# Moving the gate-times-up product of the narrow stages from one engine to two others, in their first half

## The reference, cut to what matters

```python
x = x + 0.5 * L0_ffn(layernorm(x))    # "f0", stages 0 to 7
x = x + L0_attn(layernorm(x))         # "a0"
x = x + 0.5 * L0_ffn(layernorm(x))    # "f0", stages 8 to 15
x = x + 0.5 * L1_ffn(layernorm(x))    # "f1", stages 0 to 7
x = x + L1_attn(layernorm(x))         # "a1"
x = x + 0.5 * L1_ffn(layernorm(x))    # "f1", stages 8 to 15
```

```python
def fp4_quant_dequant(x):             # blocks of 16 along the last dimension
    scale = max(max|xb| / 6, 1e-12)
    return nearest_of(0, .5, 1, 1.5, 2, 3, 4, 6)(|xb / scale|) * sign(xb) * scale
def L0_ffn(x):                        # 256 -> 704 -> 256
    gate = fp4(x) @ fp4(w_gate).T;  y = fp4(x) @ fp4(w_up).T
    h = silu(gate) * y
    return fp4(h) @ fp4(w_down).T
```

## Time and profile before

| | |
|---|---|
| median of the three runs | 2735.21 us |
| the profiled execution | 2740.86 us, its span 2739.1 us |
| busy, share of the span | PE 87%, DVE 71%, ACT 60%, POOL 32% |
| mean granted TensorE clock | 0.955 of full speed |

### The profile page before, as it was taken

The page is one execution under the profiler, slowest core; times in us unless marked ns, Lnnn a source line. Parts: engine busy times, 40 slices in busy tenths (PEclk is TensorE's granted clock), DMA queues, the critical chain, the costliest instruction groups (busy, mean ns, idle before and its releaser), DMA issues.

```text
span 2739.1 us, 55707 instructions
## 1 busy us (share of the span) xinstructions
PE 2379.6 (87%) x23228; PEld 1832.4 (67%) x23228; DVE 1951.3 (71%) x3497; ACT 1645.2 (60%) x2731; POOL 876.0 (32%) x631
## 2 busy tenths in 40 slices
PE   1778878888998999889898998989898998988888
PEld 1456656665786787667675767767666786866767
DVE  6588998999897977857677767777777656353341
ACT  2244445555867665675656566766657667665654
POOL 0112111211332423153544444353526325422212
PEclk9799999998999999999999999999899998999999
DMA  4000000000000000000000000000000000000000
GB/s 161 19 1 1 1 1 1 1 1 1 1 1 1 1 1 14 11 13 13 13 13 14 13 14 13 2 13 13 13 21 13 21 9 1 9 1 9 9 9 9
DMA packets 34842, 32.89 MB, mean 12 GB/s; under 512 B 7648, under 2 KB 33952, under 8 KB 34592
## 3 DMA queue, kind: packets, MB, share of 16 engines
q1 hardware_dynamic: 34592, 29.33, 3.2%
HBM read 12.28 MB, written 4.19 MB: 6 GB/s over the span
## 4 chain that ended last, share of the span: by engine, by line
PE 61%; DVE 22%; ACT 7%; issue 5%; POOL 2%; SPq 2%; DMA 1%; POOLq 0%; DVEq 0%; ACTq 0%
PE psum L702 16%; PE psum L703 14%; PE psum L704 14%; PE psum L708 5%; PE psum L1134 2%; PE psum L1136 2%; PE psum L1135 2%; PE psum L985 2%; PE psum L1038 2%; DVE a1pr L1867 1%; PE psum L1015 1%; SPq L677 1%; ACT a1PT L1411 1%; DVE f0sc L1689 1%; POOL a1pr L2103 1%
## 5 line engine op out<-in xcount | busy, mean ns | idle before, releaser
L2116 POOL TENSOR_TENSOR f1hT<-f1g,f1hT 128x512 f16<-128x512 f32 x256 | 308.8, 1211 | 698.2 <-ACT f1hT L1512 698.0
L2103 POOL TENSOR_TENSOR a1pr<-a1PT,a1pr 128x1024 f16<-128x1024 f32 (+1 forms) x176 | 354.2, 2015 | 306.4 <-DVE a1pr L1867 306.3
L702 PE MATMUL psum<-f1sl,f1w1h 128*128 128x256 f16 x1024 | 285.1, 278 | 18.2 <-ACT f1g L1507 8.8
L702 PE MATMUL psum<-f1w2h,f1hT 128*128 128x256 f16 x1024 | 281.1, 274 | 5.2 <-POOL f1hT L2116 3.3
L703 PE MATMUL psum<-f1sl,f1w1h 128*128 128x256 f16 x1024 | 284.4, 278 | 0.0
L704 PE MATMUL psum<-f1sl,f1w1l 128*128 128x256 f16 x1024 | 284.3, 278 | 0.0
L704 PE MATMUL psum<-f1w2h,f1hT 128*128 128x256 f16 x1024 | 280.6, 274 | 0.0
L703 PE MATMUL psum<-f1w2l,f1hT 128*128 128x256 f16 x1024 | 280.5, 274 | 0.0
L1844 DVE TENSOR_REDUCE a1nm<-psum 128x2 f32<-128x768 f32 (+3 forms) x176 | 198.0, 1125 | 72.1 <-PE psum L965 71.7
L2092 POOL TENSOR_TENSOR f0h<-f0Y,f0sc 128x704 f32<-128x704 f32 x64 | 90.2, 1409 | 465.6 <-DVE f0Y L1704 465.5
L1867 DVE CAST a1pr<-a1PT 128x1024 f16<-128x1024 f32 (+1 forms) x176 | 162.3, 925 | 59.5 <-ACT a1PT L1411 45.3
(11 more groups left out here) (335 smaller groups left out, 7099.9 us busy)
## 6 DMA issues: line engine op xcount, KB each, us to landing
a1Q<-a1st SPq DMA_DIRECT2D x96, 64.0 KB, 2.6
a1K<-a1st SPq DMA_DIRECT2D x96, 64.0 KB, 2.6
x<-in_L_attn_x SPq DMA_DIRECT2D x8, 512.0 KB, 7.8
out<-x SPq DMA_DIRECT2D x8, 512.0 KB, 2.9
wslot<-in_L_ffn_w SPq DMA_DIRECT2D x1, 1024.0 KB, 9.6
wraw<-in_L_ffn_w SPq DMA_DIRECT2D x1, 1024.0 KB, 5.6
wslot<-in_L_ffn_slot_embeds SPq DMA_DIRECT2D x1, 1024.0 KB, 7.8
a1Q<-a1mr SPq DMA_DIRECT2D x64, 4.0 KB, 1.7
```

Of the source, the lines that this page charges most:

```text
L702: e.matmul(out, lh, rh, start=start, stop=False)
L2103: e.tensor_tensor(a1["pr"][:, i % 2, 1, :, 0:w], a1["PT"][:, i % 2, :, 0:w], a1["pr"][:, i % 2, 0, :, 0:w], ALU.subtract).then_inc(s["a1_pl"])
L2116: e.tensor_tensor(hT1[:, 1, 2 * hp:2 * hp + 2, :], gg[:, hp % 2, :, :], hT1[:, 0, 2 * hp:2 * hp + 2, :], ALU.subtract).then_inc(s["f1_hl"])
```

## The change

For stages with f < B (tiles 0 to 31) the DVE multiplication at line 1685 is left out. ACT gets a new piece, due at G + 3.4: after `f0_u` and the rounding of the tile two before (`f0_hy`), it copies the up product, scaled, from banks 2 and 3 to `f0M` and signals `f0_ue`, which now frees the banks. POOL gets a new generator `f0_inner`, due at G + 4.2, which multiplies `f0M` into `f0h` and signals `f0_th`. DVE keeps the waits on `f0_si` and `f0_u` at that place. For f >= B the multiplication stays on DVE, with one added wait on `f0_th`.

```diff
 # tensor, f0_gate
-                            banks.after(n, "f0_th", ft + 1)
+                            banks.after(n, "f0_ue" if f < B else "f0_th", ft + 1)
 # scalar, f0_hidden, after the silu
+                    if f < B:
+                        yield G + 3.4
+                        q.wait_ge("f0_u", ft + 1)
+                        q.wait_ge("f0_hy", ft - 1)
+                        e.activation(f0["M"][:, t % 2, :].rearrange("p (i n) -> p i n", i=2), psum[:, 2:4, 0:FH], ACT.Copy,
+                                     scale=1.0 / (XS * WS)).then_inc(s["f0_ue"])
 # vector, f0_hidden
                     yield G + 3.8
                     q.wait_ge("f0_si", ft + 1)
                     q.wait_ge("f0_u", ft + 1)
-                    e.scalar_tensor_tensor(h3, psum[:, 2:4, 0:FH], 1.0 / (XS * WS), h3, ALU.mult, ALU.mult).then_inc(s["f0_th"])
+                    if f >= B:
+                        q.wait_ge("f0_th", ft)
+                        e.scalar_tensor_tensor(h3, psum[:, 2:4, 0:FH], 1.0 / (XS * WS), h3, ALU.mult, ALU.mult).then_inc(s["f0_th"])
 # gpsimd, new
+            def f0_inner(f):
+                S = at_f0(f)
+                for t in range(NT):
+                    ft = 4 * f + t
+                    h = f0["h"][:, ft % 3, :]
+                    yield S + 10.0 + 10.0 * t + 4.2
+                    q.wait_ge("f0_si", ft + 1)
+                    q.wait_ge("f0_ue", ft + 1)
+                    e.tensor_tensor(h, f0["M"][:, t % 2, :], h, ALU.mult).then_inc(s["f0_th"])
...
+                  chain(f0_inner, B), *[chain(z, B) for z in (a0_powers, a1_powers, a1_probs)],
```

More of the change, by code:

```diff
@@ L2119, in gpsimd @@
             return [weights(), *[chain(z, 2 * B) for z in (f0_powers, f0_products, f0_hidden)],
-                  *[chain(z, B) for z in (a0_powers, a1_powers, a1_probs)],
+                  chain(f0_inner, B), *[chain(z, B) for z in (a0_powers, a1_powers, a1_probs)],
                   *[chain(z, 2 * B) for z in (f1_powers, f1_mlp)]]
```

## The result

The changed kernel took 2785.4 us (median; 2781.8 to 2788.2) beside 2736.6 for the kernel before: a ratio of 1.0189, 95% interval 1.0166 to 1.0212. Forecast was 2721 with a range up to 2748. It is slower by 49 us, outside the range, and of the other sign.

A forecast was written before the change was run, and what follows sets the result against it. DVE was taken to bound the kernel from 120 to 630 us. Removal 24.3 less port 9.0 leaves 15.3 us, of which 14 arrive: 2735.2 - 14 = 2721 us, range 2702 to 2748.

The forecast's parts named there:

- Where DVE is bound: 120 to 630 us, f0 beside a0: DVE waits 37.3 us, 7% of the stretch, so is taken for 93%.
- nine tenths of the sum arrive: Last step: a thinner DVE list waits a little more elsewhere, so 14 of 15.3 us saved reach the time.
- The cost on ACT: 32 copies of 128x704 from PSUM at 0.75 us, 24 us in all, covered by ACT's idle time.
- POOL's duration: 32 products of 128x704 from SBUF at 1.39 us, 44 us more on POOL, hidden; nearest row up to 1766 ns.
- The port: POOL products hold up DVE instructions reading two SBUF tensors, and the cast: 0.30 us each, 9.0 us, ends 0 and 33.
- rival 1: The port takes it back: each new product costs DVE 0.8 us, 24 us in all, giving 2735; chance 0.20.
- 24.3 us removed: Line 1685 leaves DVE's list for 30 tiles in the full stretch, at 0.81 us each.
- The chain: Up product to line 1689 grows 1.3 to 1.4 us per tile, hidden if DVE has other work; counted at nothing.
- Rival 2: DVE waits for POOL at line 1689 in each tile: 27 us slower, 2762, deciding from 0.51 us a tile; chance 0.13.
- The gain at the banks: ACT frees banks 2 and 3, where PE waited 6.7 + 3.1 us for line 1685; counted at nothing.
- The order behind: Stages after 630 us: time won earlier moves all that follows forward, if their order stays as it is.
- rival 3: Planner rewrites wide stages after 630 us: eight table loads more or fewer, 10 us, 2711 or 2731; chance 0.12.

The follow-up runs named there:

- e5: Kernel before, own order: for f < B DVE's product done on 16 of 704 columns only, nothing added on ACT or POOL; 2724.0 us beside 2730.9.
- e6: Kernel before, own order, product still on DVE: ACT's copy added for f < B, DVE's product waits for it; 2740.4 us, ratio 1.0043.
- e8: Changed kernel with planner delays after ACT 129 for 130 and DVE 108 for 110, lowest planned end of 182 tries; 2695.0 us, ratio 0.9875.
- e2: Instructions of the kernel before (product on DVE) in the order the planner wrote for the changed kernel; 2780.1 us, ratio 1.0178.
- e1: Instructions of the changed kernel, every engine keeping the order of the kernel before; 2763.1 us, ratio 1.0119.
- e7: As e6, plus a POOL product of 128x704 whose result nobody uses, ACT's absolute value waiting for it; 2755.4 us, ratio 1.0096.
- e3: Changed kernel with the planner's delay after an ACT instruction moved from 130 to 131, giving another order; 2733.4 us, ratio 1.000.
- e11: Kernel before with the planner stopped after two rounds of its ten; 2748.0 us, ratio 1.0061.

## Why the prediction was wrong

**Where DVE is bound.** Right in the rows, and wrong in what followed. DVE had something to issue for 93% of the stretch, but taking 22 us out of it (e5) won 7 in the timed runs, and at most 17. The step "from its 7% of waiting I take that nine tenths of the sum arrive" failed first, though by the traces it may hold nearly (17 of 22).

**The cost on ACT.** Its duration was right (0.757 for 0.75 us). Whether its cover was there is not shown: e6 lost 5 to 9 us where nothing was counted, but with a wait of DVE for the copy that the change does not have.

**POOL's duration.** 1.39 us was taken from a product whose second operand is a small scale repeated; two whole tiles took 1.68. The stated ceiling of 1766 ns held for the median, not for single ones (2224).

**The port.** Mis-sized: 9.0 us forecast, 16.0 more in the records of the changed kernel, 17.7 beside the new product, 0.59 us for each where 0.30 was taken. That is three quarters of rival 1's price of 0.8, and it does not go away with a better order (18.2 us in e8). Of the 24.3 us removed 8 are left by this term alone, and 3 when the changed kernel is set beside e2, which has its order. The mechanism was right; the kind of DVE instruction was drawn too narrowly. "No others" than those with two tensors from SBUF and the cast is not what the rows say: the old line 1657 scales a tile of 128x32 in place, has one tensor input, and took up to 874 ns in the kernel before and 1619 in the changed one, where its median is 182. It and its like are also why the prediction found 10.1 us of excess and the whole list has 13.3.

**The chain.** Counted at nothing, and together with the port this turned the sign of the narrow stretch. The example of a silu nine microseconds old was not the rule: POOL's product was awaited at line 1697 for 13.4 us, six times and up to 4.5 us, and for 23.7 us in e1. Rival 2 named the place. Its threshold of 0.51 us of added waiting per tile goes with a port term of 9; with 16.0 it is (24.3 - 16.0) / 30 = 0.28, and 14.9 / 30 = 0.50 passed it. Its full price of 27 us was not paid in the changed kernel; e1 paid 29, by less waiting and more port than rival 2 had. In e8 the wait is 0.8 us, so it belongs to the order and not to the change as such. The gain at the banks was real and worthless: the waits of 6.7 and 3.1 us in the earlier trace rows became 2.0 for ACT's copy and 0.6 for DVE's own product of the later tiles, and PE was not last.

**The order behind.** This holds most of the miss by e2, 46 of 49 us, and 22 by e1. The prediction had it as rival 3, "pieces after 630 us may come out in another order", and sized it by table loads at plus or minus 10 us. The size was wrong by a factor of over four and the quantity was not the right one: the changed kernel has fewer table loads (177 for 184), and loses by the balance of its two lanes. It also missed that the search need not finish. The rows of a trace could not have given this number, but the planner's own figure had 36 us of it, 2735 against 2699, and the code told that it exists: any change of pieces draws a new order, and the spread of such draws was the widest term of all.

**What the change is worth.** In the same order it costs 2 to 5 us (e2 to the changed kernel, where the order was written for it) or 29 us (before to e1, where it was not). With the best order found for each there is no difference (2695.0 and 2695.4), though the narrow stretch itself is 11 us longer with the change. No run shows it ahead by more than that.

**What stays open.** Why 22 us less work on DVE brought only 7 us by the medians of e5. What the copy costs on ACT without e6's added wait. How the 32 us by which e1's waits and port meetings exceed those of e7 (23.4 and 8.6) split between the longer product on POOL and the early arrival of DVE. Why the changed kernel's two rounds gave 2735 and those of e3, one nanosecond away, 2686, is not explained either: e11 gives the cost of two rounds for the kernel before, 15 us, and not what makes one draw of two rounds better than another.

## What to carry to other kernels

Where a planner writes the order, a change is two things, and they have to be timed apart: hold the order and change the work, hold the work and change the order, and know how far a meaningless nudge moves the time (here 52 and 11 us for one nanosecond). Look at the planner's own figure before the chip runs. If it tracks the chip, as here within some 3 us for four orders of the old work and 16 us for three of the new, searching over nudges is worth more (1.3%) than the change. And moving work from DVE to POOL removes it from DVE only in part: price it with the longer POOL instruction, with the DVE instructions that it will hold up, taken from the whole list of records above their median and not from a few lines, and with whether DVE has anything to do until it is done.

## What the runs showed of the hardware that was not expected

A product of 128x704 f32 on POOL took 1362 ns with one tile as both inputs (e7), 1386 with a repeated scale as the second, and 1679 with two whole tiles. A DVE cast of 128x128, 227 ns alone, took up to 1701 ns beside POOL:

```profile
L1779 DVE CAST a0a<-a0af x32: 226/227/1701, 191.8 to 629.0; 128x128 f16<-128x128 f32 x32
```

The Trainium skill ("SBUF — State Buffer", section "SBUF: two separate sides") lets the side that starts second block fully; this row agrees: the cast began at 333.98 us, 0.06 after a POOL product of 1.67, and nearly the whole of that product was added to it. Very small instructions are held up too: beside a POOL product that began at 406.09 us, a DVE scaling of 128x4, 170 ns alone, began at 406.15 and took 1641 ns (line 1641 of the changed kernel).

Beyond the last touched instruction, e1 kept its distance to before between 21 and 24 us from 560 to 2150 us, over thousands of instructions, and at 16 to 18 from 2370 us on: with the order held, the two traces stay that close, and a difference in a late stage then points back to where it arose.
